# Softmax-pass scan factors in two PSUM banks, gathered columns three to a bank, and an edge fill in four pieces

## Chip, cores and metric

The kernel runs on one core of a Trainium2 chip. The metric is device time in microseconds (us) of one execution.

## What is computed

A graph of 3125 nodes with 32 features and 53125 edges, sorted by destination (self loops included), goes through four layers, each followed by a residual sum and a layer norm: GAT with 4 heads and a GRU, a Chebyshev filter (two sum passes) followed by GATv2 with one head, a spline convolution, and AGNN. Only GATv2 and AGNN matter here. In short:

```python
# GATv2, one head
e = leaky_relu(fsrc[src] + fdst[dst], 0.2)
logits = e @ attn
# AGNN
logits = beta * sum(x_norm[dst] * x_norm[src])
# both
mx = segment_max(logits, dst)
ex = exp(logits - mx[dst])
out = segment_sum(ex[:, None] * value[src], dst) / segment_sum(ex, dst)
```

## The kernel before

The edges lie on 125 partitions, T = 425 to a partition, in order of destination. A pass over the edges goes in CH = 17 chunks of L = 25 edges per partition; the passes are `gat`, `cheb0`, `cheb1`, `gatv2` and `agnn`. Buffers alternate by chunk (index `b`).

The source row of each edge reaches the chunk's buffer `rows` in two ways. For 11 of its 25 columns (13 in `gat`) GpSimd (POOL) issues an indirect DMA per column, lines 648 and `run_pass`; it may start chunk k only once DVE has used the rows of chunk k-2 (`rows_used`, set by the multiply of line 1542). For the other 14 columns TensorE (PE) multiplies one-hot matrices with the table of nodes (line 763, `gather_rows`), 15 matmuls to a column, into PSUM; DVE makes four of the five one-hots (line 1173, `more_hots`), ACT the fifth (lines 972 and 975), and DVE picks the right fifth of each column out of PSUM with five `copy_predicated` (line 1207, `take_half`). The columns come in two halves, 6 and 8 of them: the second half of chunk k is taken in step k, the first half of chunk k+1 at the end of step k. PE may write a half again only once it has been taken (`half_taken`).

In step k of `softmax_pass` (DVE, line 1493) the order on DVE is: a part of the edge fill (`more_fill`), the second half of the chunk's columns with four one-hots for chunk k+2 between them, the logits, a running maximum by a scan (line 1523), two differences and a sum (lines 1529 to 1532), then a wait for ACT. ACT takes two exponentials, the weights into PSUM (line 1003) and the scan factors in place in `rw` (line 1004), and releases DVE with the second; then it spreads the factors over the 33 columns of `keep` (line 1007) in SBUF. DVE meanwhile multiplies the rows by the weights (1542), copies the weights as a 33rd column (1545), adds in the carry of the chunk before (1551), waits for `keep_ready` and runs one segmented sum scan over 33 x 25 = 825 elements (`scan_chunk`, 1479), whose factors are `keep`. ACT turns the result for the store (1013, 1015).

The edge fill spreads the destination's row over all its edges in `edges_d`: one scan for each of the 32 features and each piece of the T edges (`fill_edges`, line 1406), with the marks `same` as factors. The marks stand in PSUM, copied whole at the start of each softmax pass (line 1497). The pieces are FILLS; the first (75 edges) is filled before step 0 (`start_fill`), the second (150) in steps 1 to 3, the third (200) in steps 4 to 9. In `gat` the width is 4, not 32, and all is filled before step 0.

The sum passes `cheb0` and `cheb1` have the layout to which the change brings the other two: six columns in banks 0 and 1, eight in banks 2 to 5, the scan factors in banks 6 and 7, and two scans of 400 elements (`scan_sums`, 1488). There ACT writes the factors into PSUM by two copies of 16 x 24 elements (1038). Before the change `gatv2` and `agnn` have their 14 columns two to a bank, in banks 0 to 6, and the marks, two buffers of weights and the attention vector in bank 7.

## Time and profile before

| | us |
|---|---|
| median of 3 runs (2536.48 to 2537.2) | 2537.11 |
| the profiled execution, own time | 2538.81 |
| its span, first to last instruction | 2537.1 |
| softmax pass gatv2, first to last sum scan | 1213.1 to 1485.8 |
| softmax pass agnn, first to last sum scan | 2227.5 to 2479.8 |
| busy in the span: PE | 1942.4 |
| DVE | 1836.8 |
| POOL | 1704.3 |
| ACT | 899.3 |

Each share of busy time is an average over stages that have different limits. A chunk of a pass is best read from one sum scan (line 1479) to the next: the difference of their starts is the chunk's period. In the timeline an idle stretch stands in square brackets behind the instruction that ended it, with the one that released it.

### The profile page before, as it was taken

The page shows a single profiled execution, that of the slowest core. Times are in us where ns is not written, and L with a number is a line of the kernel's source. Part 1 is how long each engine was busy: PE and PEld are TensorE (multiplying, and loading weights), DVE is VectorE, ACT ScalarE, POOL GpSimd, SP SyncE. Part 2 cuts the span into 40 slices and gives each one's busy share as a digit, 9 for nine tenths or more (in the row PEclk, how much of TensorE's full clock was granted, in tenths as well). Part 3 has the DMA queues.
Part 4 walks back from the last instruction along what each step waited for, and adds up shares of the span by engine and source line. Part 5 has one row for each costly group of instructions (what it writes and reads, how often), then busy time and mean ns, then how long its engine had stood idle before and what let it go on. Part 6 is the DMA issues. An engine that isn't in the chain of part 4 may idle for free.

```text
span 2537.1 us, 51142 instructions
## 1 busy us (share of the span) xinstructions
PE 1942.4 (77%) x20449; PEld 1701.2 (67%) x20449; DVE 1836.8 (72%) x4471; ACT 899.3 (35%) x906; POOL 1704.3 (67%) x1620
## 2 busy tenths in 40 slices
PE   2778777369994799966889946787788878589990
PEld 2777777259994799956888932455455545589990
DVE  7699998356554465534999863788887887699976
ACT  1377776334543245522444524000000000144542
POOL 6777775347775677756567751777777776567773
PEclk7888888579997899967999965899999999799995
DMA  6233333212221222213222215122211111332221
GB/s 231 69 114 113 114 120 110 76 39 75 67 73 45 52 74 67 67 23 141 80 61 57 61 31 238 49 50 50 50 49 50 50 50 41 134 87 67 68 62 21
DMA packets 83508, 194.79 MB, mean 77 GB/s; under 512 B 30864, under 2 KB 49624, under 8 KB 79554
## 3 DMA queue, kind: packets, MB, share of 16 engines
q1 hardware_dynamic: 31650, 139.14, 15.2%
q0 software_dynamic: 51744, 54.17, 11.6%
q8 instruction: 67, 1.10, 0.2%
q14 instruction: 47, 0.39, 0.0%
HBM read 107.89 MB, written 85.32 MB: 76 GB/s over the span
## 4 chain that ended last, share of the span: by engine, by line
PE 28%; POOL 25%; DVE 24%; issue 13%; ACT 6%; DMA 4%; ACTq 0%; POOLq 0%; DVEq 0%; SPq 0%
PE ps L763 25%; POOL edges_d L648 18%; DVE edges_d L1479 5%; POOL rows L648 3%; DVE rows L1207 3%; DVE edges_d L1406 3%; ACT scan L1015 3%; POOL agg L648 2%; DVE edges_d L1542 2%; PE ps L933 2%; POOL starts_dram L651 2%; DVE bigT L1479 1%; ACT edges_d L1000 1%; DVE agg L1173 1%; DMA starts_dram<-scan 1%
## 5 line engine op out<-in xcount | busy, mean ns | idle before, releaser
L648 POOL DMA_INDIRECT edges_d<-tab_y_dram,attr x425 | 433.9, 1021 | 183.5 <-issue 129.2
L763 PE MATMUL ps<-nodes,edges_d 125*128 125x160 bf16 x7140 | 498.4, 234 | 60.5 <-DVE nodes L1448 39.1
L763 PEld LDWEIGHTS ps<-nodes,edges_d 125*128 125x128 bf16 x7140 | 498.1, 98 | 61.1 <-DVE nodes L1448 39.5
L763 PE MATMUL ps<-nodes,aggn 125*128 125x180 bf16 (+2 forms) x3546 | 394.3, 244 | 117.5 <-DVE rows L1207 60.2
L648 POOL DMA_INDIRECT rows<-tab_cheb_dram,src_i x374 | 382.0, 1022 | 148.8 <-issue 113.3
L833 PE MATMUL ps<-edges_d,scan 125*125 125x480 bf16 x1700 | 364.8, 372 | 106.4 <-DVE edges_d L1947 106.4
L1207 DVE COPY_PREDICATED rows<-picks,ps 125x192 f32<-125x192 uint16 (+4 forms) x880 | 352.4, 402 | 122.1 <-PE ps L763 98.6
L833 PEld LDWEIGHTS ps<-edges_d,scan 125*125 125x125 bf16 x1700 | 228.3, 137 | 243.9 <-DVE edges_d L1947 110.7
L763 PE MATMUL ps<-nodes,agg 125*128 125x180 bf16 (+2 forms) x3564 | 339.1, 245 | 61.6 <-DVE rows L1207 61.1
L763 PEld LDWEIGHTS ps<-nodes,aggn 125*128 125x128 bf16 x3546 | 291.8, 101 | 124.0 <-issue 63.5
L763 PEld LDWEIGHTS ps<-nodes,agg 125*128 125x128 bf16 x3564 | 286.3, 101 | 67.3 <-DVE rows L1207 54.9
L648 POOL DMA_INDIRECT rows<-tab_dram,src_i x209 | 250.1, 1197 | 82.2 <-issue 59.1
L648 POOL DMA_INDIRECT rows<-tab_fsrc_dram,src_i x176 | 199.5, 1134 | 85.6 <-issue 50.6
L648 POOL DMA_INDIRECT rows<-tab_x_dram,src_i x176 | 192.5, 1094 | 70.4 <-issue 51.2
L1123 ACT ACTIVATE agg<-prod 125x160 bf16<-125x160 f32 x85 | 28.6, 337 | 547.1 <-DVE prod L1936 547.1
L763 PE MATMUL ps<-nodes,smallT 125*128 125x160 bf16 (+1 forms) x2214 | 200.6, 237 | 0.0
L1925 DVE TENSOR_TENSOR edges_d<-edges_d 125x640 f32<-125x640 f32 x85 | 70.7, 832 | 133.3 <-DMA edges_d<-tab_y_dram,attr 133.0
L763 PEld LDWEIGHTS ps<-nodes,smallT 125*128 125x128 bf16 x2214 | 167.0, 99 | 0.0
L1034 ACT ACTIVATE bigT<-rows 125x800 f32<-125x800 f32 x34 | 54.3, 1596 | 302.8 <-DVE idle L1673 302.8
L1921 DVE TENSOR_SCALAR scan<-nodes,codes 125x625 bf16<-125x625 f16 x340 | 143.5, 438 | 0.0
L1000 ACT ACTIVATE bigT<-rows 125x800 f32<-125x800 f32 x34 | 56.3, 1657 | 227.3 <-DVE rows L1207 223.8
L651 POOL DMA_INDIRECT starts_dram<-scat,start_i x75 | 78.2, 1043 | 79.3 <-DVE scat L1989 28.1
(362 smaller groups left out, 3109.1 us busy)
## 6 DMA issues: line engine op xcount, KB each, us to landing
src<-srcT_dram SPq DMA_DIRECT2D x70, 437.5 KB
scan_dram<-scan SPq DMA_DIRECT2D x17, 1700.0 KB
scan_dram<-scan SPq DMA_DIRECT2D x34, 425.0 KB
tab_y_dram<-edges_d SPq DMA_DIRECT2D x5, 2880.0 KB, 8.2
scanD_dram<-scan SPq DMA_DIRECT2D x34, 400.0 KB
starts_dram<-scan SPq DMA_DIRECT2D x2, 3400.0 KB, 13.9
edges_d<-tab_y_dram,attr POOLq DMA_INDIRECT x425, 2.6
src<-srcT_dram SPq DMA_DIRECT2D x18, 375.0 KB
```

The source lines that it names most:

```text
L648: pool.indirect_dma_start(o, None, table, bass.IndirectOffsetOnAxis(index, 0)).then_inc(s, SLOT)
L651: pool.indirect_dma_start(table, bass.IndirectOffsetOnAxis(index, 0), rows_, None, bounds_check=last, oob_is_err=False).then_inc(scattered ...
L763: ins = pe.matmul(column_ps(name, i), hots_[b][lot][:, i * NP:i * NP + P], parts_[:, part, at:at + PICKS * w], start=(lot == 0 and part == 0),
L833: ins = pe.matmul(ps[0:NP, lot, 0:PICKS * 3 * D], lot_hots[c][:, t, lot, :], picked[c][:, t, :, :].rearrange("p k c -> p (k c)"), start=(b ...
L1000: nc.scalar.activation(z[b][:, at:at + D, :], r[:, :, 0:D].rearrange("p t f -> p f t"), ACT.Copy).then_inc(rows_flipped, 1)
L1015: nc.scalar.activation(to, of, ACT.Copy).then_inc(rows_turned, 1)
L1034: nc.scalar.activation(z[b], rows[0:NP, b, 0:L * D].rearrange("p (t c) -> p c t", c=D), ACT.Copy).then_inc(rows_used, 1)
L1207: ins = vec.copy_predicated(taken, over(mask, w), half_ps(name, half, cols, pick))
L1406: ins = vec.tensor_tensor_scan(ed[:, t0:t1, c], same_ps[:, t0:t1], ed[:, t0:t1, c], ed[:, t0 - 1, c:c + 1] if i else 0.0, ALU.mult, ALU.add)
L1479: ins = vec.tensor_tensor_scan(flat, keep[:, c:c + width, :].rearrange("p c t -> p (c t)"), flat, 0.0, ALU.mult, ALU.add)
L1921: vec.tensor_scalar(lot_hots[c][:, t, :, :].rearrange("p l c -> p (l c)"), nodes16[:, 0:LOTS * NP], codes[:, c, t:t + 1], None, ALU.is_equal)
L1925: vec.tensor_tensor(slot, slot, over(basis[:, bass.ds(t0 + c * LS, LS), :], D), ALU.mult)\
```

## The change

Only for `gatv2` and `agnn`: the first six gathered columns stand three to a bank in banks 0 and 1, and the other eight in banks 2 to 5. The scan factors move from SBUF to PSUM, 20 of the 33 columns in bank 6 and 13 in bank 7 (`head_keeps`); the one ACT copy of line 1007 becomes two. Bank 7 also holds the weights, now in one buffer, the attention vector and the marks of one piece of the fill at a time. ACT now exponentiates the factors first (own semaphore `factors_made`), writes the 13 columns of bank 7, and with that copy releases DVE; the 20 columns of bank 6 follow and set `keep_ready`. DVE runs two sum scans, over 500 and 325 elements, through `scan_parts`, which `sum_pass` uses too.

For all three softmax passes the whole copy of the marks is gone and FILLS has four pieces: 75, 125, 125 and 100 edges. They are filled before step 0 and in steps 1 to 3, 4 to 8 and 9 to 13. In `gat` the fill reads its marks from SBUF; in the other two a copy puts the marks of the piece into PSUM before its first scan.

```diff
         first_in = sem("first_in")
-        edges_in = [sem("edges_in0"), sem("edges_in1"), sem("edges_in2")]
+        edges_in = [sem("edges_in0"), sem("edges_in1"), sem("edges_in2"), sem("edges_in3")]
         local_in = sem("local_in")
...
         keep_ready = sem("keep_ready")
+        factors_made = sem("factors_made")
         chunk_scanned = sem("chunk_scanned")
...
         ORDER = list(PASSES)
-        FILLS = [(0, 3 * L), (3 * L, 9 * L), (9 * L, T)]
+        FILLS = [(0, 3 * L), (3 * L, 8 * L), (8 * L, 13 * L), (13 * L, T)]
...
         columns_ps = ps[:, :, :].rearrange("p b c -> p (b c)").rearrange("p (i c) -> p i c", c=256)
-        tight_ps = ps[:, 0:2, 0:3 * PICKS * D].rearrange("p b (s c) -> p b s c", s=3)
+        def tight_ps(name):
+            w = PICKS * GATHERED[name]
+            return ps[:, 0:2, 0:3 * w].rearrange("p b (s c) -> p b s c", s=3)
...
-            if name not in ("cheb0", "cheb1"):
+            if name == "gat":
                 return columns_ps[:, i, 0:PICKS * GATHERED[name]]
             if i < 6:
-                return tight_ps[:, i // 3, i % 3, :]
-            return columns_ps[:, i - 2, 0:PICKS * D]
+                return tight_ps(name)[:, i // 3, i % 3, :]
+            return columns_ps[:, i - 2, 0:PICKS * GATHERED[name]]
...
             w = GATHERED[name]
-            if name not in ("cheb0", "cheb1"):
+            if name == "gat":
                 return columns_ps[0:NP, cols[0]:cols[-1] + 1, pick * w:(pick + 1) * w]
...
                 return columns_ps[0:NP, cols[0] - 2:cols[-1] - 1, pick * w:(pick + 1) * w]
-            return tight_ps[0:NP, :, :, pick * w:(pick + 1) * w]
+            return tight_ps(name)[0:NP, :, :, pick * w:(pick + 1) * w]
+        IN_FIRST = 20
+        head_keeps = [ps[0:NP, 6, 0:IN_FIRST * L].rearrange("p (c t) -> p c t", t=L),
+                      ps[0:NP, 7, 0:(HG - IN_FIRST) * L].rearrange("p (c t) -> p c t", t=L)]
+        marks_ps = ps[0:NP, 7, 384:512]
         HALF_D = D // 2
...
-            bank, at = (6, 256 * b) if heads > 1 else (7, 425 + L * b)
+            bank, at = (6, 256 * b) if heads > 1 else (7, (HG - IN_FIRST) * L)
             return ps[0:NP, bank, at:at + heads * L].rearrange("p (h t) -> p h t", t=L)
-        att_ps = ps[0:NP, 7, 425 + 2 * L:425 + 2 * L + D]
+        att_ps = ps[0:NP, 7, (HG - IN_FIRST + 1) * L:(HG - IN_FIRST + 1) * L + D]
...
-                filled, taken, dve_hots, last_hots = Count(), Count(), Count(), Count()
+                filled, taken, dve_hots, last_hots, made_n = Count(), Count(), Count(), Count(), Count()
...
                         nc.scalar.activation(weights_ps(b, heads), rw[:, b, 1, 0:heads, :], ACT.Exp)
-                        nc.scalar.activation(rw[:, b, 0, 0:heads, :], rw[:, b, 0, 0:heads, :], ACT.Exp)\
-                            .then_inc(act_for_vec, 1)
-                        act.wait_ge(act_for_vec, value.up())
-                        nc.scalar.activation(
-                            keep.rearrange("p (h g) t -> p h g t", g=HG)[:, :, :, 1:L],
-                            rw[:, b, 0, 0:heads, 1:L].unsqueeze(2).broadcast_to([NP, heads, HG, L - 1]),
-                            ACT.Copy).then_inc(keep_ready, 1)
+                        if heads == 1:
+                            nc.scalar.activation(rw[:, b, 0, 0, :], rw[:, b, 0, 0, :], ACT.Exp).then_inc(factors_made, 1)
+                            act.wait_ge(factors_made, made_n.up())
+                            for part in reversed(head_keeps):
+                                ins = nc.scalar.activation(
+                                    part[:, :, 1:L],
+                                    rw[:, b, 0, 0, 1:L].unsqueeze(1).broadcast_to([NP, part.shape[1], L - 1]), ACT.Copy)
+                                ins.then_inc(act_for_vec if part is head_keeps[1] else keep_ready, 1)
+                            value.up()
+                        else:
+                            nc.scalar.activation(rw[:, b, 0, 0:heads, :], rw[:, b, 0, 0:heads, :], ACT.Exp)\
+                                .then_inc(act_for_vec, 1)
+                            act.wait_ge(act_for_vec, value.up())
+                            nc.scalar.activation(
+                                keep.rearrange("p (h g) t -> p h g t", g=HG)[:, :, :, 1:L],
+                                rw[:, b, 0, 0:heads, 1:L].unsqueeze(2).broadcast_to([NP, heads, HG, L - 1]),
+                                ACT.Copy).then_inc(keep_ready, 1)
                         last_hot(k + 2, b, name)
...
                     per = SLOT * (L - PE_COLS[name])
-                    chunks(act, [(arg, 2), (value, 2), (scanned, 2), (stored[0], SLOT), (stored[1], SLOT),
+                    chunks(act, [(made_n, 2 if heads == 1 else 0), (arg, 2), (value, 2), (scanned, 2), (stored[0], SLOT), (stored[1], SLOT),
                                  (gathered[0], per), (gathered[1], per), (taken, 4), (dve_hots, 2), (last_hots, 2)], step)
...
                         mask = picks[:, b, pick, cols[0]:cols[-1] + 1]
-                        if name in ("cheb0", "cheb1") and not half:
+                        if name != "gat" and not half:
                             taken = taken.rearrange("p (b s) c -> p b s c", s=3)
...
-                same_ps = ps[0:NP, 7, 0:T]
                 def edges_view(width):
...
                     ed, (t0, t1) = edges_view(width), FILLS[i]
+                    marks = same[:, t0:t1] if width == H else marks_ps[:, 0:t1 - t0]
                     if cs[0] == 0:
                         vec.wait_ge(edges_in[i], edges_n.at())
+                        if width != H:
+                            vec.tensor_copy(marks, same[:, t0:t1]).then_inc(vec_done, 1)
+                            settle()
                     for c in cs:
-                        ins = vec.tensor_tensor_scan(ed[:, t0:t1, c], same_ps[:, t0:t1], ed[:, t0:t1, c],
+                        ins = vec.tensor_tensor_scan(ed[:, t0:t1, c], marks, ed[:, t0:t1, c],
                                                      ed[:, t0 - 1, c:c + 1] if i else 0.0, ALU.mult, ALU.add)
...
                     if width == H:
-                        for i in (1, 2):
+                        for i in range(1, len(FILLS)):
                             fill_edges(i, width, range(width))
...
                         return
-                    for i, k0, k1 in ((1, 1, 3), (2, 4, 9)):
+                    for i, k0, k1 in ((1, 1, 3), (2, 4, 8), (3, 9, 13)):
                         if k0 <= k <= k1:
...
                     vec.memset(z[1][:, :, L - 1:L], 0.0)
-                    for part in keeps_ps if name in ("cheb0", "cheb1") else [keep]:
+                    for part in keeps_ps if name in ("cheb0", "cheb1") else [keep] if name == "gat" else head_keeps:
                         vec.memset(part[:, :, 0:1], 0.0)
...
-                def scan_sums(z, b):
-                    for i, part in enumerate(keeps_ps):
-                        flat = z[b][:, i * HALF_D:(i + 1) * HALF_D, :].rearrange("p c t -> p (c t)")
+                def scan_parts(z, b, factors):
+                    c = 0
+                    for part in factors:
+                        flat = z[b][:, c:c + part.shape[1], :].rearrange("p c t -> p (c t)")
                         ins = vec.tensor_tensor_scan(flat, part.rearrange("p c t -> p (c t)"), flat,
                                                      0.0, ALU.mult, ALU.add)
+                        c += part.shape[1]
                     ins.then_inc(chunk_scanned, 1)
...
                     start_scans(name)
-                    vec.tensor_copy(same_ps, same[:, :])
                     take_half(0, 1, 0, name, lead_columns, 0, 0)
...
                         vec.wait_ge(keep_ready, kept.up())
-                        scan_chunk(z, keep, b)
+                        if heads == 1:
+                            scan_parts(z, b, head_keeps)
+                        else:
+                            scan_chunk(z, keep, b)
                         take_half(k + 1, 1 - b, 0, name)
...
                         settle()
-                        scan_sums(z, b)
+                        scan_parts(z, b, keeps_ps)
                         vec.wait_ge(rows_used, used.at(-1))
```

## Rows read from the trace of the kernel before

**Rows 1.** The page: its head and the busy times of the engines.

```profile
span 2537.1 us, 51142 instructions
PE 1942.4 (77%) x20449; PEld 1701.2 (67%) x20449; DVE 1836.8 (72%) x4471; ACT 899.3 (35%) x906; POOL 1704.3 (67%) x1620
```

**Rows 2.** Waits of DVE in gatv2 (first two) and agnn: total us, times, longest.

```profile
DVE rows L1207 <- DMA rows<-tab_fsrc_dram,src_i: 8.0, 5, 3.1
DVE bigT L1542 <- ACT rw L1004: 6.9, 17, 0.4
...
DVE rows L1207 <- PE ps L763: 13.9, 6, 3.7
```

**Rows 3.** Timeline of DVE, gatv2 from scan 4 to scan 5: start, us, instructions.

```profile
1288.77 1.88 DVE L1479 TENSOR_TENSOR_SCAN bigT<-bigT 125x825 f32<-125x825 f32 x1
...
1292.42 2.73 DVE L1406 TENSOR_TENSOR_SCAN edges_d<-ps,edges_d 125x200 f32<-125x200 f32 x5
...
1304.81 0.99 DVE L1542 TENSOR_TENSOR bigT<-bigT,ps 125x800 f32<-125x800 f32 x1 [0.41 <-ACT rw L1004]
...
1306.25 1.88 DVE L1479 TENSOR_TENSOR_SCAN bigT<-bigT 125x825 f32<-125x825 f32 x1
```

**Rows 4.** Timeline of DVE, gatv2: the sum scans of steps 9, 10, 13, 14 and 16.

```profile
1377.59 1.88 DVE L1479 TENSOR_TENSOR_SCAN bigT<-bigT 125x825 f32<-125x825 f32 x1
...
1392.38 1.88 DVE L1479 TENSOR_TENSOR_SCAN bigT<-bigT 125x825 f32<-125x825 f32 x1
...
1438.75 1.88 DVE L1479 TENSOR_TENSOR_SCAN bigT<-bigT 125x825 f32<-125x825 f32 x1
...
1455.14 1.88 DVE L1479 TENSOR_TENSOR_SCAN bigT<-bigT 125x825 f32<-125x825 f32 x1
...
1485.84 1.88 DVE L1479 TENSOR_TENSOR_SCAN bigT<-bigT 125x825 f32<-125x825 f32 x1
```

**Rows 5.** Timeline of POOL, gatv2: the gather beside the scan of step 13.

```profile
1439.17 2.21 POOL L648 DMA_INDIRECT rows<-tab_fsrc_dram,src_i  x1 [0.30 <-issue]
```

**Rows 6.** Timeline of DVE in a sum pass, its pair of scans.

```profile
709.34 1.87 DVE L1488 TENSOR_TENSOR_SCAN bigT<-ps,bigT 125x400 f32<-125x400 f32 x2
```

**Rows 7.** Timeline of POOL beside the pair of scans of rows 6.

```profile
709.59 0.94 POOL L648 DMA_INDIRECT rows<-tab_cheb_dram,src_i  x1 [0.30 <-issue]
```

**Rows 8.** Timeline of ACT, gatv2, step 5: the spreading of the factors.

```profile
1304.81 0.89 ACT L1007 ACTIVATE bigT<-rw 125x792 f32<-125x792 f32 x1
```

**Rows 9.** Groups by line and shape, ACT: busy us, mean ns, idle before.

```profile
L1038 ACT ACTIVATE ps<-samec 125x384 f32<-125x384 f32 x68 | 30.6, 483 | 0.0
```

**Rows 10.** Groups by line and shape, DVE.

```profile
L1406 DVE TENSOR_TENSOR_SCAN edges_d<-ps,edges_d 125x200 f32<-125x200 f32 x68 | 37.0, 612 | 0.0
...
L1406 DVE TENSOR_TENSOR_SCAN edges_d<-ps,edges_d 125x150 f32<-125x150 f32 x68 | 29.4, 510 | 0.0
...
L1545 DVE COPY bigT<-ps 125x25 f32<-125x25 f32 x34 | 6.0, 178 | 0.0
...
L1497 DVE COPY ps<-same 125x425 f32<-125x425 f32 x3 | 1.8, 603 | 0.1
```

**Rows 11.** Timeline of DVE, gatv2: the first instruction of the edge fill.

```profile
1195.17 0.18 DVE L1416 COPY edges_d<-first_row 125x32 f32<-125x32 f32 x1 [8.57 <-DMA edges_d<-starts_dram]
```

**Rows 12.** Timeline of DVE, agnn: the sum scans of steps 9, 10, 13 and 16.

```profile
2377.17 1.88 DVE L1479 TENSOR_TENSOR_SCAN bigT<-bigT 125x825 f32<-125x825 f32 x1
...
2390.40 1.88 DVE L1479 TENSOR_TENSOR_SCAN bigT<-bigT 125x825 f32<-125x825 f32 x1
...
2436.20 1.88 DVE L1479 TENSOR_TENSOR_SCAN bigT<-bigT 125x825 f32<-125x825 f32 x1
...
2479.84 1.88 DVE L1479 TENSOR_TENSOR_SCAN bigT<-bigT 125x825 f32<-125x825 f32 x1
```

**Rows 13.** Timeline of DVE, agnn: first takes of the second half, steps 11 and 16.

```profile
2396.53 0.46 DVE L1207 COPY_PREDICATED rows<-picks,ps 125x264 f32<-125x264 uint16 x1 [2.30 <-PE ps L763]
...
2472.32 2.40 DVE L1207 COPY_PREDICATED rows<-picks,ps 125x264 f32<-125x264 uint16 x5 [3.68 <-PE ps L763]
```

## Prediction

> **What bounds the kernel.** I read the page first: PE, DVE and POOL are each busy for two thirds to three quarters of the span [rows 1], so no engine bounds all of it and the two passes that the change touches have to be read alone. I then asked who DVE waited for in them. In gatv2 it waited 8.0 us for rows of POOL's gathers and in agnn 13.9 us for PE; the wait for ACT ahead of line 1542 recurs in all 17 steps, 0.4 us each [rows 2]. Last I read the timeline from one sum scan to the next. In step 5 of gatv2 DVE goes from scan 4 at 1288.77 to scan 5 at 1306.25, 17.48 us, with one idle stretch, that 0.41 us; 2.73 us of it are fill [rows 3]. So as long as there is fill, DVE is the bound. Without fill the period falls to 14.79 us in step 10; then POOL falls behind, and steps 10 to 13 take 61.2 us, steps 14 to 16 47.1 us [rows 4]. I call S9 the start of scan 9, and so on.
>
> **Part 1: factors in PSUM, POOL's side.** A gather that meets the scan of 825 elements, both of whose inputs stand in SBUF, takes 2.21 us [rows 5]; one that meets the sum pass's pair of scans, factors in PSUM [rows 6], takes 0.94 us [rows 7]. So POOL gets back 1.27 us per chunk. Its period where it is the bound, S14 - S13 = 16.4 us [rows 4], would fall to 15.1 us. That pays only where POOL is the bound: at most the 8.0 us of waits in gatv2, nothing in agnn.
>
> **Part 2: factors in PSUM, DVE's side.** The pair of 400 takes 1.87 us for 800 elements [rows 6], the one of 825 1.88 us [rows 3]. With 25 more elements at 2.04 ns (below) the new pair takes 1.92 us: +0.05 us a step. Bounds: nothing, and 0.1 us if unequal halves overlap less.
> The Trainium skill (VectorE: DVE Perf Modes, section on the errata, "SBUF-src ops pay a fixed extra latency per instruction") gives VectorE a larger fixed cost from PSUM than from SBUF, by 62 cycles of 0.96 GHz, or 65 ns: an estimate by that page would be 0.13 us a step for two scans, 4.4 us over both passes, against my 0.05 us a step, 1.7 us. The pair [rows 6] shows none of it, so the rows decide.
>
> **Part 3: the wait for ACT.** This is the term that matters most. Today DVE is released by the exponential of the factors, and line 1007 starts in the same instant as DVE's 1542, 1304.81 [rows 8]. After the change the copy of 13 x 24 = 312 elements comes ahead of the release. A copy of 384 into PSUM takes 483 ns [rows 9], the one of 792 into SBUF 0.89 us [rows 8]: 1.0 ns an element, so 312 take 0.41 us, and with 0.04 us for the semaphore DVE waits 0.45 us longer, 0.86 us in place of 0.41. Nothing hides it: the one-hots are issued before this wait, and multiply, weight copy, carry, scan and the next takes are queued behind it; `rows_used`, for which POOL waits, comes 0.45 us later too. Bounds: 0.35 us by proportion to 384, less hand-over; 0.89 us if all 33 columns counted; the 384 row is the nearest, so 0.45. The second copy (480 elements, 0.58 us) runs beside the multiply of 0.99 us [rows 3] and is hidden; if it weren't, the scan would start later by what it overhangs. With part 2: +0.50 us in each step that DVE bounds. ACT's added 0.1 us lies in its idle time.
>
> **Part 4: the fill.** Scans of 200 and 150 elements take 612 and 510 ns [rows 10]: 2.04 ns an element and 0.20 us fixed. Back to back they overlap: five of 200 take 2.73 us, not 3.06 [rows 3], so 0.12 us of the fixed part stays. The elements are the same, the scans beyond the first piece are 96 per pass in place of 64: +32 x 0.12 = +3.9 us per pass. Four copies of marks are new: 25 elements take 178 ns, 425 take 603 [rows 10], so 0.23 to 0.28 us and 0.03 to settle: +1.2 us. What goes, the copy of 425 marks, gains nothing in gatv2 and agnn: afterwards DVE sits idle for 8.57 us until the edges' DMA [rows 11]. In gat it is hidden likewise behind the wait for the first columns, and there 4 more scans cost +0.5 us on DVE, which bounds that pass.
> Where the fill lies counts more than its size. A scan of 100 takes 0.20 + 0.20 - 0.08 = 0.33 us in a row; 26 of the 32 of the last piece fall in steps 10 to 13, with their ends 8.9 us. Steps 0 to 9 therefore lose 3.9 - 8.9 = -5.0 us of fill. The additional DMA is issued by SP behind the three others, and only later pieces wait for it: nothing. Only the order of banks changes for PE; the picks have the same sizes: nothing, as the sum passes have this layout already.
>
> **The sum, gatv2.** Up to S9: 10 x 0.50 + 1.2 - 5.0 = +1.2 us. Steps 10 to 13: 4 x (14.79 + 0.50) + 8.9 = 70.1 us, against 61.2: +8.9. DVE is then the bound at 17.5 us a step, above POOL's 15.1, so POOL enters step 14 with its full lead of two chunks. Steps 14 to 16 took 47.1 us with 6.2 us of waiting; now 47.1 - 6.2 + 1.5 = 42.4: -4.7. Together +5.4. Cross-check: 17 x 0.50 + 3.9 + 1.2 - 8.0 = +5.6. I take 5.5.
> **agnn.** Up to S9 likewise +1.2. The step without fill takes S10 - S9 = 13.23 us; from then on PE is the bound, and steps 10 to 13 took 59.0 us, 14 to 16 43.6 [rows 12]. Now steps 10 to 13 take 4 x 13.73 + 8.9 = 63.8 us, more than PE's: +4.8. Then PE catches DVE as it did before: its half for step 11 was ready 19.36 us after S9, the following ones 15.16 us apart, and the last scan came 7.52 us after the last half [rows 12, 13]. So S16 - S13 = 19.36 + 15.16 + 7.52 + 0.5 = 42.5 us: -1.1. Together +4.9.
> With gat's 0.5: **+10.9 us**. The span goes from 2537.1 to 2548.0; the profiled execution's own time was 2538.81, the median 2537.11, so the median goes to **2548.0 us**. What follows each pass hangs on its last scan and moves as a block.
>
> **Rivals.**
> *The lock frees DVE too.* Part 1 [rows 5] shows that two engines share something. If DVE's scan also had to wait for the gather in progress, half of 0.94 us on average, the move would free 0.47 us in 34 steps, 16.0 us: 2532, faster. It wins from 0.47 us a scan. Against it: scan 5 starts at 1306.25 and DVE's idle time in the step is only the 0.41 us for ACT. Chance 0.05.
> The Trainium skill (SBUF — State Buffer, section "SBUF: two separate sides") states such a rule: the port pair that VectorE and GpSimd share is an exclusive lock, whoever starts first has it and the other blocks fully. The trace shows POOL's half of it, and no delay of the scan.
> *The wait doesn't grow.* If the 13 columns came within today's 0.41 us, some 31 steps (all 17, and 14 of agnn) would lose 14 us: -3 us, 2534, no change by measurement. For it speaks only that ACT's exponentials overlap by some tens of ns. Chance 0.05.
> *The late fill is absorbed.* If the fill of steps 10 to 13 sinks into the waits for POOL and PE that were there (8.0 and 13.9 us), agnn loses its 3.7 of steps 10 to 16 and gatv2 some 3: +4 us, 2541. Against it: DVE's own work in these steps, 17.5 and 15.9 us, exceeds POOL's 15.1 and PE's 15.16. Chance 0.10.
> *The whole spreading is waited for*, because the second copy delays the scan or the first runs long: up to 0.44 us more in 31 steps, +14: 2562. Chance 0.05.
> The forecast has 0.75.
>
> **Numbers.** The forecast alone spans 2542 to 2554: wait 0.35 to 0.50 us (-3 to +2), fixed part of a scan 0.09 to 0.14 us (-2 to +1), recovery of POOL's waits 6 to 8 us, and about 2 us of agnn's lead. Reaching to the absorbed fill, the range is **2540 to 2555**; the first two rivals and the last lie outside, some 2 in 10 with the tails. A change below 0.2%, 5.1 us, can't be told from none here. Faster 0.05 (the lock and tails), same 0.11 (the second rival and most of the absorbed fill), slower 0.84.
>
> **What the profile after should show.** The idle stretch before DVE's multiply at 0.86 us, 34 times. Two scans in 1.92 us and next to them gathers of 0.94 us. Fill scans at 0.46 (125) and 0.41 us (100). No wait for POOL's rows in gatv2, a sum scan period of about 17.4 us in steps 10 to 13, and in agnn PE waits in steps 15 and 16 alone. I am wrong if the wait before the multiply stays near 0.4 us, if POOL waits remain in gatv2, or if steps 10 to 13 of agnn still run at 15.2 us.

## The result and the profile after

| | before | changed |
|---|---|---|
| median, us (5 runs each) | 2537.2 | 2551.59 |
| lowest to highest, us | 2536.48 to 2539.14 | 2550.59 to 2553.07 |
| ratio, 95% interval | | 1.0053 [1.0041, 1.0065] |
| span of the profiled execution, us | 2537.1 | 2548.9 |

The change makes the kernel slower by 0.53% (the ratio); the medians are 14.4 us apart. The profiled spans are 11.8 us apart. The two differ because the profiled execution of before was above its median, and the changed one's, with 2550.59 us, is the lowest of its five. A later comparison (e11) gave 1.0041.

The page after, head and busy times, for [rows 1]:

```profile
span 2548.9 us, 51316 instructions
...
PE 1943.0 (76%) x20449; PEld 1703.0 (67%) x20449; DVE 1846.9 (72%) x4580; ACT 901.2 (35%) x940; POOL 1677.6 (66%) x1620
```

DVE has 10.1 us more work, POOL 26.7 us less, and the kernel is slower all the same. Next the waits of DVE in gatv2 and, last line, agnn, for [rows 2]:

```profile
DVE bigT L1564 <- ACT ps L1017: 14.9, 17, 0.9
DVE rows L1226 <- PE ps L772: 1.4, 1, 1.4
...
DVE rows L1226 <- PE ps L772: 5.0, 2, 3.2
```

The 8.0 us of waits for POOL's rows are gone, those for PE in agnn fell from 13.9 to 5.0 us, and the wait for ACT rose from 6.9 to 14.9 us in each pass. Step 5 of gatv2 on DVE, for [rows 3]; line 1564 is the multiply, 1510 the sum scans:

```profile
1309.03 0.99 DVE L1564 TENSOR_TENSOR bigT<-bigT,ps 125x800 f32<-125x800 f32 x1 [0.88 <-ACT ps L1017]
...
1310.47 1.92 DVE L1510 TENSOR_TENSOR_SCAN bigT<-ps,bigT 125x500 f32<-125x500 f32 x2
```

The idle stretch grew from 0.41 to 0.88 us. ACT in the same step, for [rows 8]: the two copies of the factors start at 1308.55, one behind the other, and take 0.94 us together; the line names the shape of the first. DVE's multiply starts 0.48 us after the first copy's start, and its 0.99 us outlast the second copy.

```profile
1308.55 0.94 ACT L1017 ACTIVATE ps<-rw 125x312 f32<-125x312 f32 x2
```

Groups by line and shape, ACT and DVE, for [rows 9, 10]:

```profile
L1017 ACT ACTIVATE ps<-rw 125x312 f32<-125x312 f32 x34 | 15.0, 441 | 1.1
...
L1427 DVE TENSOR_TENSOR_SCAN edges_d<-ps,edges_d 125x125 f32<-125x125 f32 x128 | 48.9, 456 | 0.1
...
L1427 DVE TENSOR_TENSOR_SCAN edges_d<-ps,edges_d 125x100 f32<-125x100 f32 x64 | 21.3, 405 | 0.1
...
L1424 DVE COPY ps<-same 125x125 f32<-125x125 f32 x4 | 1.2, 292 | 0.0
```

POOL while DVE runs the pair of scans from 1451.56, for [rows 5]: the gathers last 0.97 and 0.94 us, and before the first of them POOL waited 2.69 us for DVE.

```profile
1451.38 0.97 POOL L657 DMA_INDIRECT rows<-tab_fsrc_dram,src_i  x1 [2.69 <-DVE bigT L1564]
1452.65 0.94 POOL L657 DMA_INDIRECT rows<-tab_fsrc_dram,src_i  x1 [0.30 <-issue]
```

The sum scans of steps 9, 13 and 16 in gatv2, for [rows 4]:

```profile
1381.78 1.92 DVE L1510 TENSOR_TENSOR_SCAN bigT<-ps,bigT 125x500 f32<-125x500 f32 x2
...
1451.56 1.92 DVE L1510 TENSOR_TENSOR_SCAN bigT<-ps,bigT 125x500 f32<-125x500 f32 x2
...
1495.27 1.92 DVE L1510 TENSOR_TENSOR_SCAN bigT<-ps,bigT 125x500 f32<-125x500 f32 x2
```

and in agnn the takes that waited for PE, steps 15 and 16, for [rows 13]:

```profile
2468.72 2.42 DVE L1226 COPY_PREDICATED rows<-picks,ps 125x264 f32<-125x264 uint16 x5 [1.80 <-PE ps L772]
2483.88 2.40 DVE L1226 COPY_PREDICATED rows<-picks,ps 125x264 f32<-125x264 uint16 x5 [3.20 <-PE ps L772]
```

The ledger by differences of scan starts, S0 being the first:

| us, changed minus before | forecast | measured |
|---|---|---|
| gatv2, end of cheb1 to S0 | in the next row | 116.77 - 115.91 = +0.9 |
| gatv2, S0 to S9 | +1.2 with S0 | 165.58 - 164.45 = +1.1 |
| gatv2, S9 to S13 | +8.9 | 69.78 - 61.16 = +8.6 |
| gatv2, S13 to S16 | -4.7 | 43.71 - 47.09 = -3.4 |
| agnn, S0 to S9 | +1.2 with S0 | 150.17 - 149.65 = +0.5 |
| agnn, S9 to S13 | +4.8 | 63.69 - 59.03 = +4.7 |
| agnn, S13 to S16 | -1.1 | 42.60 - 43.64 = -1.0 |

These rows add up to +11.4 us. The passes cheb0 and cheb1 kept their 230.4 us from first to last scan, gat its 332.6. What lies between the passes moves from one profile to the next: the first scan of gat starts at 114.9 to 117.3 us over the thirteen profiles, and from gatv2's last scan to agnn's first it is 741.68 us before, 740.13 changed, and 740.2 to 745.9 in e1 to e8. This is why the passes, and not the spans, are compared below. The stretch from cheb1 to S0 is steadier, 115.9 to 116.4 us in the nine profiles without the longer wait, so that its +0.9 counts.

### The profile page after: what moved, and what is told of

Same layout as the page of the kernel before. It is cut to its first block, busy times and chain, and to the rows that moved or that the text cites. A ratio compares the mean times of both kernels' runs of the same rounds, so it can differ in the third digit from the quotient of the medians.

```text
span 2548.9 us, 51316 instructions
## 1 busy us (share of the span) xinstructions
PE 1943.0 (76%) x20449; PEld 1703.0 (67%) x20449; DVE 1846.9 (72%) x4580; ACT 901.2 (35%) x940; POOL 1677.6 (66%) x1620
## 4 chain that ended last, share of the span: by engine, by line
DVE 29%; PE 26%; POOL 22%; issue 13%; ACT 6%; DMA 3%; DVEq 0%; ACTq 0%; POOLq 0%; SPq 0%
PE ps L772 23%; POOL edges_d L657 18%; DVE edges_d L1500 5%; DVE rows L1226 4%; DVE edges_d L1427 3%; POOL agg L657 3%; ACT scan L1034 3%; DVE bigT L1510 2%; DVE edges_d L1564 2%; PE ps L942 2%; POOL starts_dram L660 2%; ACT edges_d L1009 1%; DVE agg L1192 1%; DVE smallT L1192 1%; DMA starts_dram<-scan 1%
## 5 line engine op out<-in xcount | busy, mean ns | idle before, releaser
L657 POOL DMA_INDIRECT rows<-tab_fsrc_dram,src_i x176 | 183.8, 1044 | 105.0 <-DVE bigT L1564 55.7
L657 POOL DMA_INDIRECT rows<-tab_x_dram,src_i x176 | 183.6, 1043 | 80.4 <-issue 49.4
L1510 DVE TENSOR_TENSOR_SCAN bigT<-ps,bigT 125x400 f32<-125x400 f32 (+2 forms) x136 | 129.0, 990 | 2.5 <-DVE bigT L1573 0.2
## 6 DMA issues: line engine op xcount, KB each, us to landing
starts_dram<-scan SPq DMA_DIRECT2D x2, 3400.0 KB, 13.9
```

The lines of the kernel that those rows point to most:

```text
L657: pool.indirect_dma_start(o, None, table, bass.IndirectOffsetOnAxis(index, 0)).then_inc(s, SLOT)
L1510: ins = vec.tensor_tensor_scan(flat, part.rearrange("p c t -> p (c t)"), flat, 0.0, ALU.mult, ALU.add)
```

## Experiments

Time of each pass from S0 to S16, read from the timelines as above, and the ratio to before, all of them timed on the same chip as the runs of before they are divided by:

| | gatv2 | agnn | ratio, 95% interval |
|---|---|---|---|
| before | 272.70 | 252.32 | |
| changed | 279.07 | 256.46 | 1.0053 [1.0041, 1.0065] |
| e1: pieces alone | 271.96 | 248.41 | 0.9985 [0.9975, 0.9995] |
| e2: release after both copies | 286.85 | 263.09 | 1.0106 [1.0089, 1.0123] |
| e3: weights in SBUF, early release | 271.95 | 249.93 | 0.9993 [0.9983, 1.0002] |
| e4: columns alone | 272.82 | 252.33 | 0.9999 [0.9989, 1.0008] |
| e5: e3 with old pieces | 270.58 | 253.71 | 1.0006 [0.9996, 1.0015] |
| e6: changed with old pieces | 274.93 | 258.35 | 1.0041 [1.0027, 1.0055] |
| e7: e3, marks in SBUF | 272.14 | 250.54 | 1.0011 [1.0001, 1.0020] |
| e8: pieces 75, 225, 125 | 269.49 | 253.02 | 0.9985 [0.9975, 0.9995] |
| e9: pieces by pass | 269.33 | 249.41 | 0.9966 [0.9952, 0.9979] |
| e10: e5 with e8's pieces | 269.33 | 253.71 | 0.9979 [0.9968, 0.9990] |
| e11: changed again | 279.00 | 256.51 | 1.0041 [1.0028, 1.0054] |

The pass times of the changed kernel repeat within 0.07 us (e11), and e9's gatv2 repeats e8's within 0.2 us, so a pass resolves differences that a whole run doesn't. The last steps of agnn are an exception: e9 has e1's pieces there and came out at 249.41 in place of 248.41 us, all of it from S13 to S16. Only one trace of before exists, and the runs were made on three chips (e1 to e4, e5 to e8, e9 to e11).

**e1, the pieces alone.**

```diff
...
-        FILLS = [(0, 3 * L), (3 * L, 9 * L), (9 * L, T)]
+        FILLS = [(0, 3 * L), (3 * L, 8 * L), (8 * L, 13 * L), (13 * L, T)]
...
-                    for i, k0, k1 in ((1, 1, 3), (2, 4, 9)):
+                    for i, k0, k1 in ((1, 1, 3), (2, 4, 8), (3, 9, 13)):
```

> The kernel before with only the fill in four pieces (75, 125, 125, 100), marks still whole in PSUM. My theory: 32 more scans of 0.12 us fixed part in each pass, but 8.9 us of the fill move from steps 1 to 9, where DVE is the bound, to steps 10 to 13, where it waits for POOL or PE. gatv2 -3.4 us, agnn -3.8 us, gat +0.5 us: about -7 us, 2530. Rival (the fill is what made the changed kernel slower): the extra scans and the four late steps cost at least +4 us in each pass, 2545 or more.

Faster, ratio 0.9985, but by 3.8 us and not by 7. agnn -3.9 us, as expected; gatv2 only -0.7 in place of -3.4. There S0 to S9 gave 159.77 - 164.45 = -4.7 us and S9 to S13 68.11 - 61.16 = +6.9, which is what the prediction's arithmetic gives without the longer wait (4 x 14.79 + 8.9 = 68.1). S13 to S16, where 6.2 us of waits for POOL went, gave only -3.0. The waits of DVE in gatv2 say why:

```profile
DVE bigT L1542 <- ACT rw L1004: 6.9, 17, 0.4
...
DVE rows L1207 <- PE ps L763: 3.2, 2, 1.8
```

No wait for POOL is left in gatv2, but once it is gone PE is late in the last steps. (In agnn one new wait for POOL's rows appears, 4.1 us in the last step, where DVE before waited for PE.) And it is gone although factors and scans are where they were: the late fill alone gave POOL the time. The rival falls: the fill by itself doesn't make this kernel slower.

**e2, a longer wait.** The changed kernel with the release of DVE moved behind the second copy.

```diff
-                            for part in reversed(head_keeps):
+                            for part in head_keeps:
...
-                                ins.then_inc(act_for_vec if part is head_keeps[1] else keep_ready, 1)
+                            ins.then_inc(act_for_vec, 1)
...
-                        vec.wait_ge(keep_ready, kept.up())
+                        if heads > 1:
+                            vec.wait_ge(keep_ready, kept.up())
```

> The changed kernel with DVE released only after both copies of the factors (the 20 columns first, then the 13), so that the suspected wait is made longer by about 0.49 us a step and nothing else is changed. My theory (the wait for ACT is on the path of every step that DVE bounds): the idle stretch before the multiply is 1.35 us in place of 0.87, and the time goes up by 0.49 us in 31 to 34 steps: +15 to +17 us over the changed kernel, about 2567. Rival (the wait is beside other work, POOL or PE set the pace): under +5 us.

```profile
DVE bigT L1564 <- ACT ps L1017: 22.1, 16, 1.4
```

The wait is 22.1 / 16 = 1.38 us, 0.50 us more, and the passes take 7.8 and 6.6 us more than in the changed kernel, 14.4 us in all, a little under the range. From S0 to S16 there are 16 periods in each pass; 14.4 us for 0.50 us is 29 of these 32. In agnn, where DVE still waits 4.0 us for PE in its last two steps, it is 13 of 16.

**e3, the wait taken away.** The changed kernel with the weights of the two passes in SBUF, in place in `rw`. Bank 7 then holds nothing that DVE needs before the scan, and the exponential of the factors can release DVE.

```diff
-            bank, at = (6, 256 * b) if heads > 1 else (7, (HG - IN_FIRST) * L)
-            return ps[0:NP, bank, at:at + heads * L].rearrange("p (h t) -> p h t", t=L)
+            if heads == 1:
+                return rw[:, b, 1, 0:1, :]
+            return ps[0:NP, 6, 256 * b:256 * b + heads * L].rearrange("p (h t) -> p h t", t=L)
...
-                            nc.scalar.activation(rw[:, b, 0, 0, :], rw[:, b, 0, 0, :], ACT.Exp).then_inc(factors_made, 1)
-                            act.wait_ge(factors_made, made_n.up())
+                            nc.scalar.activation(rw[:, b, 0, 0, :], rw[:, b, 0, 0, :], ACT.Exp).then_inc(act_for_vec, 1)
+                            act.wait_ge(act_for_vec, value.up())
...
```

> The changed kernel with the weights of gatv2 and agnn in SBUF, so that DVE can be released by the exponential of the factors again, ahead of both copies. My theory: the idle stretch before the multiply goes back to 0.41 us and 0.46 us come back in 31 to 34 steps: -14 to -15 us from the changed kernel, 2536 to 2538. The multiply now has both inputs in SBUF, so the gathers beside it are held up by some 0.4 us; that costs nothing while DVE is the bound. Rival (the two scans, the new bank layout or the marks cost the time, not the wait): less than 5 us come back.

```profile
DVE bigT L1564 <- ACT rw L1015: 6.9, 17, 0.4
```

The wait is back at 6.9 us, the passes at 271.95 and 249.93: 7.1 and 6.5 us less than in the changed kernel, 13.6 us for 0.47 us, again 29 of 32 periods. Together, e2 and e3 bracket the wait from both sides with the same slope, and the rivals of both fall.

**e4, the columns alone.** The kernel before with `tight_ps`, `column_ps`, `half_ps` and the mask of the changed kernel, nothing else.

```diff
-        tight_ps = ps[:, 0:2, 0:3 * PICKS * D].rearrange("p b (s c) -> p b s c", s=3)
+        def tight_ps(name):
+            w = PICKS * GATHERED[name]
+            return ps[:, 0:2, 0:3 * w].rearrange("p b (s c) -> p b s c", s=3)
...
-            if name not in ("cheb0", "cheb1"):
+            if name == "gat":
...
-                        if name in ("cheb0", "cheb1") and not half:
+                        if name != "gat" and not half:
```

> The kernel before with only the columns of gatv2 and agnn moved to three in a bank. My theory: the matmuls and the picks have the same sizes and the same order, so no difference, within 2 us of before. Rival (picks out of a bank that holds three columns, or PE that writes one bank for longer, cost something): takes of the first half longer than 0.37 us a pick, 3 us or more over before.

272.82 and 252.33 us against 272.70 and 252.32: the order of the columns in the banks costs and gives nothing, as expected.

**e5, POOL's relief alone.** As e3, with the old pieces, and marks read from SBUF since the pieces of 150 and 200 don't fit into bank 7.

```diff
...
-        FILLS = [(0, 3 * L), (3 * L, 8 * L), (8 * L, 13 * L), (13 * L, T)]
+        FILLS = [(0, 3 * L), (3 * L, 9 * L), (9 * L, T)]
...
-                    marks = same[:, t0:t1] if width == H else marks_ps[:, 0:t1 - t0]
+                    marks = same[:, t0:t1]
...
-                        if width != H:
-                            vec.tensor_copy(marks, same[:, t0:t1]).then_inc(vec_done, 1)
-                            settle()
...
-                    for i, k0, k1 in ((1, 1, 3), (2, 4, 8), (3, 9, 13)):
+                    for i, k0, k1 in ((1, 1, 3), (2, 4, 9)):
```

> Factors in PSUM as in the changed kernel, weights in SBUF (release by the exponential, as in e3), but the fill in the three old pieces with marks read from SBUF. Against the kernel before, the factors' place is the one thing left that can pay. My theory (part 1 of the prediction): gathers beside the scan take 0.94 us, not 2.21, those beside the multiply some 0.4 us more; POOL's period where it is the bound falls by 0.9 us, and of the 8.0 us of waits in gatv2 about 5 go; agnn, bound by PE, +0 to +1. Total -4 us against before. Rival (only the late fill took the waits away, as e1 did with factors in SBUF): waits for POOL's rows stay at 6 us or more, total 0 to +2.

```profile
DVE rows L1226 <- PE ps L773: 3.7, 2, 1.9
```

All waits for POOL's rows in gatv2 are gone, more than I expected, and 3.7 us for PE have taken their place. So the relief is real and would have been enough by itself to remove them. But the -4 us in all was missed, and the total lies where the rival put it: the pass gained 2.1 us, not 5, agnn lost 1.4, and in all nothing can be told from before. In gatv2 S13 to S16 gave -4.0 us, but S0 to S9 +1.9 us, of which 0.45 us are the longer pair of scans and 1.0 us the first one-hots after each part of the fill, which now reads its marks from SBUF (see the last section); some 0.4 us aren't located.

**e6, the changed kernel with the old pieces,** the wait for ACT kept and marks read from SBUF.

```diff
...
-        FILLS = [(0, 3 * L), (3 * L, 8 * L), (8 * L, 13 * L), (13 * L, T)]
+        FILLS = [(0, 3 * L), (3 * L, 9 * L), (9 * L, T)]
...
-                    marks = same[:, t0:t1] if width == H else marks_ps[:, 0:t1 - t0]
+                    marks = same[:, t0:t1]
...
-                    for i, k0, k1 in ((1, 1, 3), (2, 4, 8), (3, 9, 13)):
+                    for i, k0, k1 in ((1, 1, 3), (2, 4, 9)):
```

> The changed kernel with the fill in the three old pieces and marks read from SBUF; the longer wait for ACT stays. My theory: +0.5 us in each step that DVE bounds, less the waits for POOL in gatv2: gatv2 +0.5 us (0 to 9 +5.0), agnn +5.5 us (0 to 9 +5.0, then PE sets the pace), in all +6 us over before, about 8 us under the changed kernel. Rival (with the pieces' order undone the changed kernel gets slower, since e1 showed that the late pieces pay): more than the changed kernel's +13 us.

gatv2 +2.2 and agnn +6.0 us against before (+0.5 and +5.5 expected), +8.3 in all, 2.3 us under the changed kernel; the rival falls, and my theory had gatv2 wrong. Between whole runs the two can't be told apart (1.0041 and 1.0053, intervals that overlap). S0 to S9 gave +5.8 and +5.6 us, S13 to S16 -3.4 and -0.1 us. With the longer wait DVE sets the pace nearly throughout gatv2. There it doesn't matter in which step a part of the fill lies, and the changed kernel's four pieces, with 32 more scans and the copies of marks, cost 4.1 us; in agnn, where PE sets the pace late, they still give 1.9 us.

**e7, marks of the four pieces in SBUF.** As e3, without the copies into PSUM.

```diff
-                    marks = same[:, t0:t1] if width == H else marks_ps[:, 0:t1 - t0]
+                    marks = same[:, t0:t1]
...
-                        if width != H:
-                            vec.tensor_copy(marks, same[:, t0:t1]).then_inc(vec_done, 1)
-                            settle()
```

> As e3 (weights in SBUF, four pieces), but the marks of the fill are read from SBUF, without the four copies into PSUM per pass. My theory: the copies are on DVE's path, 1.2 us a pass, and fill scans last the same from SBUF: -2 to -2.5 us against e3. Rival (fill scans with both inputs in SBUF hold POOL up so far that it becomes the bound): no gain, and waits for POOL's rows in gatv2 or agnn of 3 us or more.

No gain: 272.14 and 250.54 us against e3's 271.95 and 249.93. The rival was right in the result and wrong in the reason: no wait for POOL's rows appeared. Groups by line, DVE:

```profile
L1424 DVE TENSOR_TENSOR_SCAN edges_d<-same,edges_d 125x125 f32<-125x125 f32 x136 | 52.7, 466 | 0.1
```

The scans of 125 last 466 ns in place of 457, those of 100 411 in place of 405, together 0.8 us over the 96 scans of a pass. The first one-hots after each part of the fill last 0.73 us on the mean in gatv2 and 0.78 in agnn, where e3 has 0.68 and 0.67; over 13 steps that is another 0.7 and 1.4 us. The two eat up what the copies had cost.

**e8, three pieces of 75, 225 and 125 on the kernel before.**

```diff
-        FILLS = [(0, 3 * L), (3 * L, 9 * L), (9 * L, T)]
+        FILLS = [(0, 3 * L), (3 * L, 12 * L), (12 * L, T)]
...
-                    for i, k0, k1 in ((1, 1, 3), (2, 4, 9)):
+                    for i, k0, k1 in ((1, 1, 3), (2, 4, 12)):
```

> The kernel before with only the pieces changed: 75, 225 and 125 edges, the last filled in steps 4 to 12; no additional scans. My theory: steps 1 to 3 take 4.8 us more, steps 4 to 9 9.4 us less, steps 10 to 12 4.2 us more, which falls into waits for POOL and PE. gatv2 about -5 us, agnn -4.6 us: -9 to -10 us, 2528, about twice what e1 gained. Rival (more fill in steps 1 to 3 starves PE or waits for the longer edge transfer): no better than e1, -4 us.

```profile
DVE rows L1207 <- DMA rows<-tab_fsrc_dram,src_i: 4.9, 3, 3.1
...
DVE rows L1207 <- PE ps L763: 14.9, 12, 3.7
```

gatv2 -3.2 us, still with 4.9 us of waits for rows (first line). agnn +0.7 us: DVE waits for PE 12 times (second line), not 6. The additional fill in steps 1 to 3 holds up the takes: from S0 to S3 PE is idle for 8.1 us of 58.2 (5.4 of 53.4 before), and from S3 to S13 it is busy without a gap, so that the lost time doesn't come back. The -9 to -10 us were missed by far; in all the ratio is e1's, as the rival said, and for agnn its reason, a starved PE, is seen too.

**e9, pieces by pass on the kernel before:** e8's in gatv2, e1's in agnn, the old ones in gat.

```diff
...
-        FILLS = [(0, 3 * L), (3 * L, 9 * L), (9 * L, T)]
+        CUTS = {"gat": (3, 9), "gatv2": (3, 12), "agnn": (3, 8, 13)}
+        FILLS = {n: list(zip((0,) + tuple(c * L for c in cs), tuple(c * L for c in cs) + (T,)))
+                 for n, cs in CUTS.items()}
...
-                    for i, k0, k1 in ((1, 1, 3), (2, 4, 9)):
+                    for i, k0, k1 in {"gatv2": ((1, 1, 3), (2, 4, 12)), "agnn": ((1, 1, 3), (2, 4, 8), (3, 9, 13))}[name]:
```

> The kernel before with pieces chosen for each pass and nothing else: gatv2 as in e8 (75, 225, 125 up to step 12), agnn as in e1 (75, 125, 125, 100 up to step 13), gat as before. My theory (what pays is how much of the fill falls into steps in which DVE waits, and each pass has its own such steps): from scan 0 to scan 16 gatv2 -3.2 us, agnn -3.9 us as measured apart, in all -7 us, ratio 0.997, faster than both kernels. Rival (the gains of e1 and e8 are drift between runs and don't add): -4 us or less.

gatv2 -3.4, agnn -2.9 us; ratio 0.9966 [0.9952, 0.9979]. This version beats both kernels. The medians are 6.2 us apart, the two passes give 6.3 us, and the ratio stands for 8.7, with an interval of 5.4 to 12.2; the rival, 4 us or less, falls. agnn gained a microsecond less than in e1, where its last step waited 4.1 us for POOL's rows, here 5.1.

**e10, all together:** e5 with the pieces of e8.

```diff
-        FILLS = [(0, 3 * L), (3 * L, 9 * L), (9 * L, T)]
+        FILLS = [(0, 3 * L), (3 * L, 12 * L), (12 * L, T)]
...
-                    for i, k0, k1 in ((1, 1, 3), (2, 4, 9)):
+                    for i, k0, k1 in ((1, 1, 3), (2, 4, 12)):
```

> As e5 (factors in PSUM, weights and marks in SBUF) with the pieces of e8. My theory: in gatv2 the relief of POOL takes away e8's last 4.9 us of waits for rows, but fill from SBUF costs 1.3 us (e5) and the scan pair 0.05 us a step: gatv2 -4 us against before, agnn +2 us (PE is starved in steps 1 to 3 as in e8); -2 us in all. Rival (the relief is worth more than its price): -5 us or better, under e8.

269.33 us in gatv2, as e9 without factors in PSUM: POOL's relief pays for its own price and no more. agnn +1.4 us. The passes give -2.0 us in all, as expected; the ratio, 0.9979, is 5.4 us, where the rival stood. Its interval, 2.6 to 8.2 us, doesn't reach down to 2.0, and the traces don't show where the rest comes from. Since gatv2 and agnn are the passes that the relief can reach, I go by them.

**e11, the changed kernel again.**

> The changed kernel once more. The first comparison gave 11.8 us between the two profiled spans and 14.4 us between the medians; the passes gatv2 and agnn accounted for 6.4 and 4.1 us from scan 0 to scan 16. My theory: these two figures repeat within 0.5 us, the start of each pass adds 0.7 to 0.9 us, and what lies beyond (the start of gat, the spline layer) differs from execution to execution: in all +12 to +14 us. Rival (something outside the passes got slower by the change): the first scan of gat or the stretch from gatv2 to agnn is late again by 2 us or more against before.

The passes repeat; cheb1's last to gatv2's first scan is 116.76 us (116.77 in the first profile, 115.91 before). The first scan of gat comes at 115.48 us, against 114.92 before and 116.84 in the first profile of the change, so that start was chance and not the change. From gatv2's last scan to agnn's first it is 757.21 us here and 740.13 in the first profile of the same kernel. Most of that isn't the change: e9 and e10, on the chip of e11, have 755.34 and 754.79 us there, and the runs of before had a median of 2551.66 on it. The 1.9 to 2.4 us that remain are within what this stretch moves by on the other chips, so the rival is neither borne out nor excluded for it.

## Why the prediction was right, and where it wasn't

The forecast was +10.9 us, the medians show +14.4, the profiled spans +11.8, and the passes with gatv2's start +11.4. The direction and the mechanism came as forecast. That the sum is so near is in part luck: gatv2 came out 1.8 us above its +5.4 (+0.8 up to S9, -0.3, +1.3), agnn 0.7 us below its +4.9, and gat's +0.5 isn't in the 11.4. The 3 us between the passes and the medians aren't located.

- **Part 3, the wait for ACT: right, and the term that decides.** 0.45 us forecast, 0.47 measured (0.88 - 0.41). e3 takes it away and 13.6 us come back; e2 adds 0.50 us and 14.4 are lost. The wait alone, taken away, turns the change from a loss into no change (e3, 0.9993).
- **Part 2: right.** The pair takes 1.92 us, as forecast, and by this case's rows the larger fixed cost from PSUM doesn't show: 1.92 us for 825 elements against 1.88 from SBUF.
- **Part 4: right in size.** Scans of 125 and 100 take 456 and 405 ns (0.46 and 0.41 forecast), copies 0.29 us (0.28). Steps 10 to 13 gave +8.6 for +8.9 in gatv2 and +4.7 for +4.8 in agnn. gat's +0.5 us isn't shown: its first scan started at 116.84 us in one profile of the changed kernel and at 115.48 in the other.
- **Part 1: the mechanism right, its credit wrong.** I wrote that POOL's relief pays up to the 8.0 us of waits in gatv2, and then, in the sum, I booked their return under the slower DVE. Both are true and neither is needed for the other: the late fill alone removes the waits with factors in SBUF (e1), the relief alone removes them with the old fill (e5). In the changed kernel they are paid for twice. The 1.27 us a chunk were read from one gather: it holds in steps 10 to 14, but from S0 to S16 all gathers of gatv2 together took 187.4 us before and 172.2 changed, 0.95 us a chunk (the last section says why).
- **agnn, steps 14 to 16: right.** PE caught up as forecast: the half for step 15 was ready 19.5 us after S13 (19.36 forecast), the next one 15.16 us later, S16 came 8.0 us after that; 42.6 us in all for 42.5.
- **gatv2, steps 14 to 16: mis-sized.** -3.4 us in place of -4.7. The forecast had DVE free of any wait there; PE is late by 1.4 us in the changed kernel, 3.2 in e1 and 3.7 in e5. The step that failed is "47.1 - 6.2 + 1.5": behind POOL the next bound, PE, lies 1 to 4 us away, and I had not looked for it in gatv2.
- **Rivals.** The wait grew (e2, e3), so the second falls; the late fill wasn't absorbed in the changed kernel, so the third falls, though without the longer wait it is in part (e1: of its 8.9 us, S9 to S16 show 1.0 in agnn and 3.9 in gatv2); the second copy stayed hidden, so the fourth falls. The lock rival is wrong for the scan. In the kernel before, 29 of the 34 sum scans begin while a gather is under way, which runs on for 0.1 to 0.8 us; each begins 0.31 to 0.34 us after the start of the instruction before it, as the other five do, and lasts 1.88 us. DVE does feel POOL elsewhere (below).

What the change did, then: it removed 8 us of waits for POOL in gatv2, where 1.4 us for PE took their place, and 9 us for PE in agnn, by relieving POOL and by giving DVE more to do before it came to them, and made DVE the bound almost to the end of both passes, with 0.47 us more idle time in every step of its own.

## What to carry to other kernels

When data moves into a shared bank, look at who now has to wait for whom because of the bank: here the weights that DVE needs at once share bank 7 with factors that it needs later, the program releases DVE only behind ACT's copy into that bank, and 0.47 us in some 30 steps outweighed all that the move gave back. No run tried an earlier release with the weights left in bank 7. Background work such as the fill belongs into the steps in which its engine waits, and these differ by pass; e9 does only that and is the fastest version. Before a wait is booked as a gain, ask which engine is late next.

## What the hardware showed that I had not expected

- **A gather that begins beside the scan ends at a fixed time.** In the kernel before, each gather that begins during a sum scan, from 0.10 to 1.12 us after its start, ends 2.62 to 2.64 us after that start, some 0.75 us after the scan's end; [rows 5] with the scan of 1438.75 in [rows 4] is one: 1439.17 + 2.21 = 1441.38. So the delay isn't a fixed price: 1.27 us for one that begins 0.42 us after the scan, 0.6 us for one that begins after 1.09, as in most steps up to S9.
- **A one-hot on DVE can take longer beside a gather.** In e5, after a fill with marks and edges both in SBUF, the first one-hot of step 6 takes 0.87 us and the next 0.67 (DVE timeline, first lines below), beside a gather that began at 1315.45. In gatv2 of e5 the first one-hot after the fill takes 0.87 to 0.89 us in six of nine steps and 0.67 in three; in the kernel before, with marks in PSUM, 0.67 or 0.68 us in seven and 0.77 and 0.78 in two, and 0.88 once in agnn. So it isn't the marks' place by itself: what goes with the longer ones is a gather that has some 0.3 to 0.5 us left to run when they begin.

```profile
1316.29 0.87 DVE L1192 TENSOR_SCALAR agg<-src,lot_f 125x1754 bf16<-125x1754 f16 x1
1317.41 0.67 DVE L1192 TENSOR_SCALAR agg<-src,lot_f 125x1754 bf16<-125x1754 f16 x1
```

```profile
1315.45 1.28 POOL L658 DMA_INDIRECT rows<-tab_fsrc_dram,src_i  x1 [0.30 <-issue]
```

  The Trainium skill (SBUF — State Buffer, section "SBUF: two separate sides") says that whichever of the two starts first holds the pair of ports that VectorE and GpSimd share for its whole instruction and the other blocks fully. These rows agree with it in part: the one-hot takes 0.20 us longer, but the gather before it ran on for 0.44 us after the one-hot's start. The sum scan, which reads two inputs in SBUF, took 1.88 us in all 34 steps of before and only POOL was held up. Why the one and not the other wasn't tried apart.
- **A copy into PSUM on ACT:** 312 elements take 441 ns, 384 take 483 and 480 take 567; the proportional guess from 384 to 312 (0.39 us) would have been too low by 0.05 us, the prediction's 0.41 by 0.03.
